# Seeding the accumulation bank of a gated delta-rule recurrence from ScalarE instead of with an identity matmul

## The reference

```python
def step(S, ins):
    q_t, k_t, v_t, a_t, b_t = ins
    read = jnp.einsum('bhk,bhkv->bhv', k_t, S)
    err = read - v_t
    S = a_t[:, :, None, :] * S - b_t[:, :, None, None] * k_t[..., None] * err[:, :, None, :]
    o_t = jnp.einsum('bhk,bhkv->bhv', q_t, S)
    return (S, o_t)
```

## Time and profile before

| | |
|---|---|
| runs shown | 1932.83, 1935.91, 1937.22 us; median 1935.91 |
| the profiled execution | 1919.19 us, of it a span of 1917.1 us |
| granted TensorE clock over the span | 0.972 of full speed |
| TensorE busy | 1703.5 us (89%), 15702 matmul records |
| its weight loads | 1445.2 us (75%) |
| VectorE busy | 1362.2 us (71%) |
| ScalarE busy | 1000.8 us (52%) |
| GpSimd busy | 619.1 us (32%) |
| recurrence | from about 69 to 1049 us |

### The profile page before, as it was taken

The page is one execution under the profiler, slowest core; times in us unless marked ns, Lnnn a source line. Parts: engine busy times, 40 slices in busy tenths (PEclk is TensorE's granted clock), DMA queues, the critical chain, the costliest instruction groups (busy, mean ns, idle before and its releaser), DMA issues. The chain is left out here.

```text
span 1917.1 us, 42317 instructions
## 1 busy us (share of the span) xinstructions
PE 1703.5 (89%) x15702; PEld 1445.2 (75%) x15702; DVE 1362.2 (71%) x3230; ACT 1000.8 (52%) x2618; POOL 619.1 (32%) x975
## 2 busy tenths in 40 slices
PE   4599999899999999999988598999999999998895
PEld 3477778787877778877876365688888888888794
DVE  4688777877788777877775475566666666664777
ACT  2355555555555555565543354556566656652353
POOL 6455345543555335543451122000000000001653
PEclk9799999999999999999988799999999999999898
DMA  6212331323222332323320200990000000003232
GB/s 216 59 51 65 75 86 49 68 59 85 65 56 65 75 87 46 74 67 75 83 50 23 90 1 5 183 14 2 2 2 2 1 2 1 2 2 107 65 93 76
DMA packets 150338, 106.78 MB, mean 56 GB/s; under 512 B 34132, under 2 KB 138648, under 8 KB 149240
## 3 DMA queue, kind: packets, MB, share of 16 engines
q1 hardware_dynamic: 147640, 98.95, 23.7%
q0 software_dynamic: 2496, 5.13, 0.8%
HBM read 86.06 MB, written 17.99 MB: 54 GB/s over the span
## 5 line engine op out<-in xcount | busy, mean ns | idle before, releaser
L593 POOL TENSOR_TENSOR kfull<-kt,pair_rows 128x512 f32<-128x512 f32 x128 | 143.6, 1122 | 517.2 <-ACT kt L381 513.5
L361 PE MATMUL ps<-xT,taps 128*128 128x128 f32 x2048 | 276.8, 278 | 0.1
L853 ACT COPY wt<-ps 32x128 f32<-32x128 f32 x512 | 131.7, 257 | 263.9 <-PE ps L748 256.9
L361 PEld LDWEIGHTS ps<-xT,taps 128*128 128x128 f32 x2048 | 258.7, 196 | 7.6 <-issue 7.2
L1687 DVE TENSOR_REDUCE b_nmax<-ps 128x1 f32<-128x128 f32 (+7 forms) x256 | 180.6, 752 | 72.9 <-PE ps L1524 72.9
L896 DVE TENSOR_TENSOR prod<-ps,mt 128x128 f32<-128x128 f32 x512 | 147.4, 288 | 78.6 <-PE ps L759 62.7
L748 PE MATMUL ps<-ident,w 128*128 128x128 f32 x512 | 162.9, 318 | 34.6 <-ACT wt L853 18.5
L1664 POOL COPY b_spread<-b_inv 128x256 f32<-128x256 f32 x64 | 25.8, 402 | 513.2 <-DVE b_inv L1690 513.2
L899 DVE TENSOR_REDUCE w<-prod 128x32 f32<-128x128 f32 x512 | 146.5, 286 | 17.5
L748 PEld LDWEIGHTS ps<-ident,w 128*128 128x128 f32 x512 | 88.1, 172 | 84.9 <-DVE w L899 73.6
L1616 ACT ACTIVATE b_prob_long<-ps,b_nmax 128x1024 f32<-128x1024 f32 (+3 forms) x128 | 121.4, 953 | 55.7 <-DVE b_nmax L1687 55.7
(11 more groups left out here) (308 smaller groups left out, 3843.2 us busy)
## 6 DMA issues: line engine op xcount, KB each, us to landing
decay<-ends_dram SPq DMA_DIRECT2D x256, 128.0 KB, 5.5
gn<-near_dram SPq DMA_DIRECT2D x32, 384.0 KB, 6.9
slots_dram<-zero SPq DMA_DIRECT2D x1, 9216.0 KB, 59.3
rr<-rates_dram SPq DMA_DIRECT2D x32, 256.0 KB, 4.5
sq<-rstd_dram SPq DMA_DIRECT2D x16, 512.0 KB, 3.6
wtap<-in_taps SPq DMA_DIRECT2D x4, 1024.0 KB, 11.2
f_w<-in_f_w SPq DMA_DIRECT2D x2, 2048.0 KB, 10.4
s_xb<-slots_dram SPq DMA_DIRECT2D x46, 64.5 KB, 1.8
```

The source lines that it names most:

```text
L361: mm = pe.matmul(part, lhsT=taps[:, tap, t * P:(t + 1) * P], rhs=xT[:, :, columns(at_next) - LOOK + tap:columns(at_next) - LOOK + tap + TS ...
L593: nc.gpsimd.tensor_tensor(kfull[:, n % 4, :, :], kt[:, n % 2, :].unsqueeze(1).to_broadcast([P, G, P]), cst["pair_rows"][:, :].unsqueeze(2) ...
L853: nc.scalar.copy(wt[rows, b, :], ps[rows, 2, 0:P]).then_inc(wt_kept[b], 1)
```

## The change

Two copies on ScalarE take the place of the identity product. `preset` copies zeros (from a new one-column tile `zero`, which GpSimd sets once) into columns 128 to 255 of bank `b`, and the values into columns 0 to 127. It takes over the two waits that L730 had, and it stands in ScalarE's order between `ring(2)` and `ring(3)` of each half, for the start of the next half. For the first two starts it stands ahead of the loop. TensorE's first product with the state now waits for both copies (`z_set`) and for the state. Since every product into the bank now accumulates, banks 0 and 1 get an identity product of 512 columns once, in the preparing block, as banks 4 and 5 had already.

```diff
+        zero = sb("a_zero", [P, 1])
...
             def _(pe):
                 for b in range(B):
+                    pe.matmul(ps[:, b, :], lhsT=cst["ident"][:, :], rhs=state[:, b, :, :].rearrange("p g v -> p (g v)"),
+                              start=True, stop=True, skip_group_check=True)
                     pe.matmul(ps[:, 4 + b, :], lhsT=cst["ident"][:, :], rhs=state[:, b, :, :].rearrange("p g v -> p (g v)"),
                               start=True, stop=True, skip_group_check=True)
...
                 nc.gpsimd.memset(o[:, 1, :, :, :], 0.0)
+                nc.gpsimd.memset(zero[:, :], 0.0)
...
                 def start(cc, b):
                     f, c = cc // NC, cc % NC
-                    if c == 0 and f >= 1:
-                        pe.wait_ge(S["prepared"], 2 * f)
-                    if cc >= 1:
-                        pe.wait_ge(o_kept[b], cc)
-                    vdc = vd[:, f % 2, :, b, :].rearrange("p h (c i s) -> p c i h s", c=NC, s=BK)
-                    pe.matmul(z_of(b), lhsT=cst["ident"][:, :], rhs=vdc[:, c], start=True, stop=False,
-                              skip_group_check=True)
+                    pe.wait_ge(z_set[b], 2 * (cc + 1))
                     if cc >= 1:
                         pe.wait_ge(s_ready[b], cc)
...
+                def preset(cc, b):
+                    f, c = cc // NC, cc % NC
+                    if c == 0 and f >= 1:
+                        act.wait_ge(S["prepared"], 2 * f)
+                    if cc >= 1:
+                        act.wait_ge(o_kept[b], cc)
+                    values = vd[:, f % 2, :, b, :].rearrange("p h (c i s) -> p c i h s", c=NC, s=BK)
+                    nc.scalar.copy(ps[:, b, P:2 * P], zero[:, 0:1].to_broadcast([P, P])).then_inc(z_set[b], 1)
+                    nc.scalar.copy(z_of(b), values[:, c]).then_inc(z_set[b], 1)
+
+                preset(0, 0)
+                preset(0, 1)
...
                     keep(cc, x, 1)
                     ring(2)
+                    if cy >= 0 and cy < last_chunk:
+                        preset(cy + 1, y)
                     ring(3)
                     if cc >= 1:
                         put_back(cc - 1, x)
```

More of the change, by code:

```diff
@@ L268, in delta_attention @@
         two = lambda n: [sem(f"a_{n}{b}") for b in range(B)]
-        z_ready, w_ready, wt_ready, wt_kept = two("z_ready"), two("w_ready"), two("wt_ready"), two("wt_kept")
+        z_set, z_ready, w_ready, wt_ready, wt_kept = (two(n) for n in ("z_set", "z_ready", "w_ready", "wt_ready", "wt_kept"))
         p_ready, s_ready, s_back, o_ready, o_kept = (two("p_ready"), two("s_ready"), two("s_back"), two("o_ready"),
@@ L274, in delta_attention @@
         every = list(S.values()) + [dve_chain, pool_chain] + decay_in[0] + decay_in[1]
-        for pair in (z_ready, w_ready, wt_ready, wt_kept, p_ready, s_ready, s_back, o_ready, o_kept):
+        for pair in (z_set, z_ready, w_ready, wt_ready, wt_kept, p_ready, s_ready, s_back, o_ready, o_kept):
             every += pair
```

## The result

| | before | with the change |
|---|---|---|
| median | 1935.91 us (11 runs, 1929.53 to 1938.54) | 1940.33 us (11 runs, 1939.11 to 1943.50) |
| ratio to before, 95% interval | | 1.0031 [1.0021, 1.0040] |
| profiled execution | 1919.19 us | 1939.11 us |
| its span | 1917.1 us | 1937.4 us |

By the ratio the change is slower by 0.31%; the medians lie 4.4 us apart. The measured median lies inside its range of 1926 to 1942, but on the other side of before. Both kernels were run again later: 1.0029 [1.0018, 1.0040] for the change, 0.9993 [0.9985, 1.0002] for the kernel before against itself.

What follows compares the result with a forecast made beforehand. TensorE looked like the bound, but behind the product it still idled for VectorE's new state, so little was gained. +1.8 - 3.0 - 1.1 + 0.3 = -2.0 us on 1919.19 gave 1917.2; with 16.7 carried over, 1933.9, range 1926 to 1942.

Steps and rivals of the forecast that it cites:

- Ahead of the loop, +1.8: Preparing block: two added identity products, four passes, delay the first projection by 1.8 us, or 3.5 if slow.
- j = 1, gain 0: Start 1: the 0.31 saved on TensorE is lost after 2 us, as L759 waits for ScalarE's copy of wt.
- j = 2, gain 0: Start 2: gq waits 2.19 us for kt and the solve follows gq, not the product; gain 0 or worse.
- The pair at j = 1, 0.02 a frame: ScalarE's two copies, taken as 0.30, delay kt, gq and solve; 0.28 slack leaves 0.02 a frame, +0.3 us.
- j = 3, gain 0: Start 3: gq waits for the copy kt and the copy of wt stands behind put_back, so gain 0.
- Hidden starts j = 0, 4, 5, 0: Starts 0, 4 and 5: TensorE waits for VectorE's state after L730 is done, so removing L730 gives 0.
- j = 6 and 7, -0.2: Start 6 gains 0; start 7's solve and VectorE-GpSimd alternation come 0.2 earlier: -3.0 us over 15 frames, bounds 0 and -4.7.
- the rival: Half 7: the lock belongs to GpSimd, so no gain there; sum +1.0 us, 1936.9, inside no change, chance 0.18.
- The last frame, -1.1: Last frame, without projections: six starts, each following the update by 0.19, together gain 1.1 us; other end 0.
- The 16.7 us: Runs' median above the profiled execution before the change; unexplained by the stages, carried over into the forecast.
- ScalarE's queue, the rival on the slower side: Each frame's first iteration, near_rows to gq: pair at 0.54 costs +3.9 us; sum +3.3 to +6.3, 1942.2; chance 0.15.
- three signs of being wrong: Frame shorter by 0.5 or more, L737 waiting for ScalarE's pair, or the solve at j = 2 over 0.3 later.

Runs made afterwards that it cites:

- dve_half1: The changed kernel with half 1's pair of copies made by VectorE behind its state update instead of by ScalarE; 1941.18 us, ratio 1.0017.
- one_at_6: The changed kernel with one identity product of 128 columns into an unused bank at the start of half 6 only; 1946.19 us, ratio 1.0050.
- swap_waits: The changed kernel with the two waits ahead of L735 in the other order, state first, then seed; 1939.41 us, ratio 1.0015.
- fill_edge: The changed kernel with eight identity products of 128 columns ahead of the wait at each frame's half 0; 1936.48 us, ratio 0.9998.
- before_wait2: The kernel before with a second, already satisfied wait ahead of L737's product with the state; 1939.74 us, ratio 1.0017.

## Why the prediction was wrong

The forecast had the frame's length right to a tenth (61.0 forecast by -0.18, 61.10 measured) and the sign of the whole wrong. Step by step:

- **Ahead of the loop, +1.8: right.** 1.72 at the first projection, four passes slow and four fast as worked out; 1.3 to 1.6 at start 0.
- **j = 1, gain 0: right.** Start 1 is 0.22 earlier, and L757 behind it stands at 9.48 as in before and in all other profiles, waiting for wt.
- **j = 2, gain 0: wrong in its reason.** I had the second solve follow gq and kt. The earlier trace rows has VectorE idle 0.29 ahead of it for TensorE's L759, so it followed TensorE, and the product was on its path: 0.22 a frame, seen in dve_half1 (18.31 against 18.53). In the change the pair stands in the way of it.
- **The pair at j = 1, 0.02 a frame: mis-sized.** It puts off gq by 0.40 where I had 0.30. The slack I had nearly right, 0.26 against 0.28. So it costs 0.14 a frame against before, 2.1 us over 15 and not 0.3.
- **j = 3, gain 0: right.** L757 behind start 3 is 0.14 later than L759 was, as much as behind start 2; nothing of the product is left.
- **The size of a product.** Where TensorE sets the start, a product is worth 0.22 and not the 0.31 that I took from the spacing of L730 and L737 (5-6 in before, the change and one_at_6: 8.77, 8.55, 8.78).
- **Hidden starts j = 0, 4, 5, 0: wrong.** I costed the product and not the wait that it carried. Taking it away put two waits ahead of one instruction, and the state then reaches TensorE 0.1 later. That costs 0.19 a frame, 2.9 us over 15 (swap_waits).
- **j = 6 and 7, -0.2: about right in size, for the wrong reason.** Measured from start 5 to start 0: -0.31, with 0.1 of the second wait in it. Half 6 gained because VectorE got ahead of GpSimd, which I had ruled out by taking 0 there. At j = 7 I had let GpSimd's L543 wait for VectorE's L514, because L514 started first. It didn't: kfull held GpSimd until 434.90, and L543 started as kfull ended. So the end belongs to GpSimd, as the rival had it, L521 ends 0.47 after L544, and GpSimd, set back by 0.69 from start 6 on, takes half 7's gain.
- **The last frame, -1.1: wrong.** Where TensorE runs at 2.4 GHz there, a start follows the update by 0.15 instead of 0.19, 0.04 each, and the starts come every 5.70 instead of 5.74; the second wait ate the rest (0.06 with the waits swapped). I had counted six such starts, and only four of them ran at 2.4 GHz.
- **TensorE's clock: missing.** I had counted L730 at j = 0 as hidden, at no cost and no gain. It was the only work in TensorE's pause at the frame's edge. Without it the pause is 2.2 us, and three to four frames are 1.4 to 1.6 longer. fill_edge takes exactly this away. This, 2.8 and 4.2 us in the two pairs of profiles, is most of what separates "no change" from "slower". The frame from which the earlier trace rows come, 377.24 to 440.00, takes 62.76 and not 61.2, since it is the one with before's own stretch; I had not asked why.
- **The end of the loop: open in part.** 12.6 us against 10.5 and 11.5 after the last start, with more of it at 1.2 GHz. The same 12.5 to 12.8 stands in all other kernels, before_wait2 without any copies among them, but the two with products at the edge alone (10.0 and 12.1), so it isn't the copies. No run changed it by itself.
- **The 16.7 us** between the first profile and the median were rightly carried over as no property of the kernel: the second profile took 1937.39.

In sum: +1.8, -2.7 and -1.1 were forecast. Measured are +1.3 to +1.6 ahead of the loop, -0.1 a frame in place of -0.18, +0.6 to +2.3 for the last frame and the end, and 2.8 to 4.2 us of clock that no term stood for, less the 1.0 of the frame that turned over in before alone. That the frame came out so near is luck: +0.14 (the pair), +0.1 (the second wait, at start 5) and -0.31 (from start 5 to start 0) in place of +0.02, 0 and -0.2.

ScalarE's queue, the rival on the slower side, had its place right. Its price of 0.26 a frame is too high against before (0.14); with 0.14 the forecast's own sum would have been -0.2 us, so this rival isn't what made the kernel slower. None of the three signs of being wrong came: the frame was 0.1 shorter, L735 never waited for the pair, and the solve at j = 2 was 0.14 later. TensorE's busy time fell by 2.0 us a frame and not by 2.5 to 3. The steps that failed are the two that looked at L730 in a pause and saw nothing there: neither the clock that it kept up nor the wait that it carried.

## What to carry to other kernels

A product that runs under a wait isn't free to remove: ask what it keeps busy (the engine's clock) and which wait it carries for its neighbour. Where TensorE pauses about 2 us once in every round, cheap products in the pause can be worth more than the work that was saved. When a start has lost an instruction in front of it, measure the gain at the work behind it, not at the start. Where two waits stand ahead of one instruction, write the one that ends last first and look at the delay behind its releaser in the trace.

## What was unexpected on the chip

- **Two waits ahead of one TensorE product.** With one wait it started 0.05 us after the recorded end of VectorE's update; with a second, already satisfied wait written ahead of it, 0.15; with the same second wait written behind it, 0.06. The 0.15 is the same in both kernels, at each of the three starts; the other order was run in the change alone. Why the order matters, no run shows.
- **The clock falls behind some pauses only.** With a pause of 2.1 to 2.2 us at each edge, 3 to 5 of 14 frames had a stretch of 3.4 us at 1.2 GHz, and 8 of 14 where the frame was 60.73. With eight products in the pause there was none in three kernels. With 1.5 us of idle time and one product behind it there were five, and in one_at_6 two behind 1.8. The kernels with L730 pause for 0.66 and 1.4 to 1.5 around it in the frame that turned over: a stretch came behind that in both profiles of before and not in before_wait2. Their usual pause, split by L730 into twice 0.6, brought none.
- **Copies of 128x128 into PSUM** take 0.27 us on ScalarE and 0.28 on VectorE and follow each other after 0.19 to 0.20 on both.
- **One product of 128 columns at the right place moved a frame by 0.53 us**, of which 0.23 is the product itself; the rest came because it turned over who of VectorE and GpSimd went first.
